# A post-norm decoder layer: head loop unrolled with batches in pairs, heads' projection and half of the feed-forward beside it

## The reference

```python
q, k, v = ((x @ W).reshape(B, T, 16, 128) for W in (Wq, Wk, Wv))     # x: 4,256,256; W: 256,2048
q, k = rmsnorm(q, q_rms_w), rmsnorm(k, k_rms_w)
s = einsum('bthd,bshd->bhts', q, k) / sqrt(128) - dist * slope[h]    # causal, slope 2**-0.5 .. 2**-8
y = rmsnorm(softmax(s) @ v, subln_w)                                 # per head
x = layernorm(x + y.reshape(B, T, 2048) @ Wproj)                     # Wproj: 2048,256
a = softmax((ctx @ xWq.T + bq) @ (ctx @ xWk.T + bk).T)               # B,256,256
x = layernorm(x + x_mixed)             # x_mixed: x_b @ a_b.T, per batch (the tokens' 256 channels mixed)
g, u = bitlinear(x, w_gate), bitlinear(x, w_up)    # 1024 wide; 8-bit activations, ternary weights
x = layernorm(x + bitlinear(sigmoid(g) * u, w_down))
```

## Time and profile before

| | |
|---|---|
| median of 3 runs | 434.68 us (433.88 to 435.26) |
| profiled execution, first to last instruction (span) | 432.9 us |
| PE busy | 401.9 us (93%) |
| DVE busy | 327.7 us (76%) |
| ACT busy | 254.4 us (59%) |
| POOL busy | 220.2 us (51%) |
| first q/k/v matmul | 18.77 us |
| last head step's matmuls | to about 312 us |
| mean granted TensorE clock | 0.979 |

### The profile page before, as it was taken

How to read it: one execution, slowest core, us unless ns; L and a number is a source line. 1 busy time by engine, 2 the same in 40 slices (tenths; PEclk the granted TensorE clock), 3 DMA queues, 4 the chain that set the end, 5 groups by cost and what they waited for, 6 DMA issues and landing times.

```text
span 432.9 us, 9595 instructions
## 1 busy us (share of the span) xinstructions
PE 401.9 (93%) x2605; PEld 361.1 (83%) x2612; DVE 327.7 (76%) x1000; ACT 254.4 (59%) x750; POOL 220.2 (51%) x368
## 2 busy tenths in 40 slices
PE   4979999999999999999999999999999899999552
PEld 3668899999999999999999999999988677777321
DVE  0777987887797798788779779878822788888862
ACT  3486777677676776767767677676722333333321
POOL 3633667676675776767767677675501122222210
PEclk9999999999999999999999999999999999999965
DMA  8980010110101101011010110000000000000000
GB/s 223 316 251 2 2 36 3 38 37 0 36 0 36 36 0 36 0 36 36 0 36 0 36 36 0 0 0 0 0 2 0 2 0 15 12 14 12 13 14 24
DMA packets 21747, 14.52 MB, mean 34 GB/s; under 512 B 1760, under 2 KB 21472, under 8 KB 21728
## 3 DMA queue, kind: packets, MB, share of 16 engines
q1 hardware_dynamic: 21728, 14.29, 11.2%
HBM read 13.24 MB, written 1.05 MB: 33 GB/s over the span
## 4 chain that ended last, share of the span: by engine, by line
PE 86%; DVE 5%; ACT 4%; issue 2%; DMA 1%; POOL 1%; SPq 0%; POOLq 0%; DVEq 0%
PE ps L482 30%; PE ps L422 11%; PE ps L493 7%; PE ps L506 6%; PE ps L499 5%; PE ps L512 4%; PE ps L505 3%; PE ps L514 3%; PE ps L513 3%; PE ps L521 3%; PE ps L587 3%; PE ps L572 2%; ACT hT L696 2%; DMA x_sb<-in_x 1%; PE ps L557 1%
## 5 line engine op out<-in xcount | busy, mean ns | idle before, releaser
L315 POOL TENSOR_TENSOR qk_rstd<-qk_sum,minus_half 128x2 f32<-128x2 f32 x128 | 88.5, 692 | 92.6 <-DVE qk_sum L797 90.8
L482 PE MATMUL ps<-w_hi,xT_hi 128*128 128x384 f32 x256 | 96.9, 378 | 2.3 <-DVE qk_n L791 1.4
L482 PE MATMUL ps<-w_hi,xT_lo 128*128 128x384 f32 x256 | 86.5, 338 | 0.0
L482 PE MATMUL ps<-w_lo,xT_hi 128*128 128x384 f32 x256 | 86.3, 337 | 0.0
L797 DVE TENSOR_REDUCE qk_sum<-sq 128x2 f32<-128x258 f32 x128 | 53.6, 419 | 30.8 <-ACT sq L635 29.1
L635 ACT ACTIVATE sq<-ps 128x256 f32<-128x256 f32 x128 | 49.1, 384 | 34.6 <-PE ps L482 34.4
L791 DVE TENSOR_TENSOR qk_n<-ps,qk_rstd 128x256 f32<-128x256 f32 x128 | 54.2, 423 | 18.8 <-POOL qk_rstd L315 17.8
L422 PE MATMUL ps<-wp,yT 128*128 128x256 f32 x256 | 62.2, 382 | 0.0
L310 POOL TENSOR_TENSOR y_rstd<-y_sum,minus_half 128x2 f32<-128x2 f32 x64 | 49.0, 766 | 24.6 <-DVE y_sum L804 20.9
L673 ACT ACTIVATE sqy<-ps 128x258 f32<-128x258 f32 x64 | 24.8, 387 | 58.5 <-PE ps L514 58.5
L422 PEld LDWEIGHTS ps<-wp,yT 128*128 128x128 f32 x256 | 46.7, 190 | 5.9
(11 more groups left out here) (126 smaller groups left out, 846.9 us busy)
## 6 DMA issues: line engine op xcount, KB each, us to landing
w_raw<-in_L_attn_Wq SPq DMA_DIRECT2D x16, 128.0 KB, 2.2
w_raw<-in_L_attn_Wk SPq DMA_DIRECT2D x16, 128.0 KB, 2.3
w_raw<-in_L_attn_Wv SPq DMA_DIRECT2D x16, 128.0 KB, 2.3
wp<-in_L_attn_Wproj SPq DMA_DIRECT2D x1, 2048.0 KB, 16.1
ff_raw<-in_L_ffn_w_gate SPq DMA_DIRECT2D x1, 1024.0 KB, 8.6
ff_raw<-in_L_ffn_w_up SPq DMA_DIRECT2D x1, 1024.0 KB, 11.0
ff_raw<-in_L_ffn_w_down SPq DMA_DIRECT2D x1, 1024.0 KB, 13.0
out<-fin SPq DMA_DIRECT2D x8, 128.0 KB, 1.7
```

The costliest lines, as they stand in the source:

```text
L315: pool.tensor_tensor(qk_rstd[:, t, :], qk_sum[:, t, :], minus_half[:], ALU.pow).then_inc(s_rs[t], 1)
L482: last = pe.matmul(ps[:, t, 0:3 * D], xa[:, k, tok], wa[:, r, k * 3 * D:(k + 1) * 3 * D], start=(i == 0), stop=(i == len(parts) - 1))
```

## The change

The loop is unrolled: every body is written out for n in 0 to 68. Step n is now head n // 2 % 16 of batch 2 * (n // 32) + n % 2, so batches 0 and 1 finish all heads at step 31 and batches 2 and 3 at step 63. Each head's weights are therefore loaded and split twice (32 groups of two steps instead of 16 of four); the high parts are now made by ACT in one copy a group (`split_hi`), the low parts by POOL.

The projection is done per four heads and batch (`quad_at`): 24 fp32r matmuls of 256 columns into PSUM region 0, twelve in each of two slots, from y and Wproj split into high and low parts; DVE adds the result onto x in SBUF (`accumulate`). For this, y^T is stored as `yT_hi` (ACT) and `yT_lo` (DVE, one more instruction each step), and `wp_lo` is made by POOL.

Everything else goes into two *slots* of a body: slot 0 stands ahead of q/k/v of tile 1 on PE, after `norm(n, 0)` on DVE and between the two qk_rstd on POOL; slot 1 stands at the end of the body on PE, and on DVE, POOL and ACT near the start of the next body, on POOL ahead of y_rstd. `plan()` gives the slots: the cross attention in steps 1 to 17, one block of feed-forward weights in each of steps 6 to 29, and from step 36 the whole feed-forward of tiles 0 to 3 (batches 0 and 1), seventeen stages a tile, a tile about every seven steps. After the bodies, five rounds remain for tiles 4 to 7. The sigmoid becomes 0.5 * (1 + tanh(g / 2)), its factors folded into scales. The prologue is cut to the transposes of x of batches 0 and 1; the first loads are x of batch 0 and, on ACT's queue, the first weights.

The schedule:

```diff
+STAGES = ("st0", "x1", "t1", "xm", "x2a", "x2b", "t2", "g0", "u0", "g1", "u1", "hs", "hr", "hq", "th", "dn", "fin")
...
+            steps = [2 * H * (b // 2) + 2 * (QUAD * k + i) + b % 2 for i in range(QUAD)]
+            if steps[-1] + 5 == n:
+                return b, k, steps
...
+    for k in range(FF_UNITS):
+        put(6 + k, 0, "fquant", k)
+        put(6 + k, 1, "fturn", k)
+    slot = 2 * 36
+    for u in range(FFN_IN_LOOP):
+        for stage in STAGES:
+            while stage in IN_PSUM and slot % 2 == 0 and quad_at(slot // 2):
+                slot += 1
+            put(slot // 2, slot % 2, stage, u)
+            if stage == "th":
+                after = slot
+            slot += 1
+        slot = after
```

The body of POOL, and its new `split_lo`:

```diff
+            def split_lo(g, piece):
+                if piece == 0:
+                    pool.wait_ge(s_whi, g + 1)
                 cols = slice(piece * KC * D, (piece + 1) * KC * D)
...
+                pool.tensor_tensor(w_lo[:, g % 3, cols], w_flat(g)[:, cols], w_hi[:, g % 3, cols].bitcast(F32),
+                                   ALU.subtract).then_inc(s_split, 1)
...
+            for n in range(STEPS + 3):
+                if n > 0:
+                    side_work(n - 1, 1)
+                if n >= 3:
                     pool.wait_ge(s_ssy, n - 2)
                     wait(pool, s_yn, n - 3)
                     pool.tensor_tensor(y_rstd[:], y_sum[:], minus_half[:], ALU.pow).then_inc(s_ry, 1)
...
+                if n < STEPS:
+                    qk_rstd_of(n, 0)
+                side_work(n, 0)
+                if n < STEPS:
+                    qk_rstd_of(n, 1)
+                g = n // 2 + 2
+                if g < GROUPS:
+                    if n % 2 == 0:
+                        split_lo(g, 0)
+                        split_lo(g, 1)
+                    else:
+                        split_lo(g, 2)
+                if n % 2 == 1 and 0 <= n // 2 - 1 < H:
+                    h = n // 2 - 1
+                    pool.wait_ge(s_wphi, h // 4 + 1)
+                    pool.tensor_tensor(wp_lo[:, h, :], wp_raw[:, h // QUAD % 2, h % QUAD, :], wp_hi[:, h, :].bitcast(F32),
+                                       ALU.subtract).then_inc(s_wplo, 1)
+
+                if n % 2 == 1 and 2 <= g - 1 < GROUPS:
+                    pool.wait_ge(s_sc, 2 * (g - 3) + 2)
+                    by = 0.5 if (g - 1) % H >= 2 else 2.0 ** (H // 2 - 1)
+                    pool.tensor_scalar(bias[:, (g - 1) % 2], bias[:, (g - 1) % 2], by, 1.0, ALU.mult,
+                                       ALU.mult).then_inc(s_bias, 1)
```

PE, the projection of four heads (t is the slot):

```diff
+                for i, m in enumerate(steps):
+                    for j, (ya, wa) in enumerate(((yT_hi, wp_hi), (yT_hi, wp_lo), (yT_lo, wp_hi))):
+                        last = pe.matmul(region[0][:, t * C:(t + 1) * C], ya[:, m % RING, t * P:(t + 1) * P],
+                                         wa[:, head_of(m), :], start=(i == 0 and j == 0),
+                                         stop=(i == QUAD - 1 and j == 2))
```

The body of DVE (the instructions that were there before, such as y_sum, y_n, pT, are unchanged):

```diff
+            for n in range(STEPS + DEPTH):
+                if 0 <= n - 1 < STEPS:
+                    norm(n - 1, 1)
+                if 0 <= n - 3 < STEPS:
                     dve.wait_ge(s_sqy, n - 2)
                     wait(dve, s_ry, n - 3)
                     dve.tensor_reduce(y_sum[:], sqy[:], AX.X, ALU.add).then_inc(s_ssy, 1)
...
+                if n > 0:
+                    side_work(n - 1, 1)
+                if n < STEPS:
+                    sums(n, 0)
+                if 0 <= n - 3 < STEPS:
                     dve.wait_ge(s_ry, n - 2)
                     wait(dve, s_ty, n - 3)
                     dve.tensor_tensor(y_n[:], ps_y[:, :, 0:D], y_rstd[:].unsqueeze(2).to_broadcast([P, TT, D]),
                                       ALU.mult).then_inc(s_yn, 1)
...
+                if 0 <= n - 2 < STEPS:
                     dve.wait_ge(s_tp, n - 1)
                     wait(dve, s_y, n - 2)
                     dve.tensor_copy(pT[:], ps_pT).then_inc(s_pT, 1)
...
+                if n < STEPS:
+                    norm(n, 0)
+                side_work(n, 0)
+                if 0 <= n - 4 < STEPS:
+                    m = n - 4
+                    dve.wait_ge(s_yhi, m + 1)
+                    dve.scalar_tensor_tensor(out=yT_lo[:, m % RING, :].rearrange("p (t d) -> p t d", t=TT), in0=ps_yT,
+                                             scalar=sub_scale,
+                                             in1=yT_hi[:, m % RING, :].bitcast(F32).rearrange("p (t d) -> p t d", t=TT),
+                                             op0=ALU.mult, op1=ALU.subtract).then_inc(s_ylo, 1)
+                if n < STEPS:
+                    sums(n, 1)
...
+            for m in range(FFN_IN_LOOP, NT + 1):
```

More of the change, by code:

```diff
@@ new lines, with plan, put @@
+IN_PSUM = ("xw", "ctx", "cq", "ck", "wtotal", "energy", "cturn", "turnx", "fturn",
+           "t1", "xm", "t2", "g0", "u0", "g1", "u1", "th", "dn")
+def plan():
+    at = {}
+    def put(n, slot, stage, i):
+        at.setdefault((n, slot), []).append((stage, i))
+    put(1, 0, "xw", 0)
+    for i in range(2):
+        put(2 + i, 0, "ctx", i)
+        put(4 + i, 0, "cq", i)
+        put(6 + i, 0, "ck", i)
+    for i in range(3):
+        put(2 + i, 1, "wsum", i)
+    put(5, 1, "wtotal", 0)
+    for b, (energy, norm, turn) in enumerate(((8, 9, 10), (9, 10, 14), (13, 14, 16), (15, 16, 17))):
+        put(energy, 0, "energy", b)
+        put(norm, 0, "cnorm", b)
+        put(turn, 0, "cturn", b)
+    put(18, 0, "turnx", 2)
+    put(21, 0, "turnx", 3)
+    for k in range(FF_UNITS):
[11 more added lines that the diff above has]
+        slot = after
+    assert slot < 2 * (STEPS + DEPTH) - 2
+    return at
@@ new lines, in gate_up, with turn_hq @@
+            def gate_up(to, w, f):
+                for k in range(KC):
+                    last = pe.matmul(to, xqT[:, k, :], w[:, k, f * BANK:(f + 1) * BANK],
+                                     start=(k == 0), stop=(k == KC - 1))
+                return last
+            def turn_hq(to):
+                for f in range(FC):
+                    last = pe.transpose(to.bitcast(BF16)[:, f * P:(f + 1) * P], hq[:, f * P:(f + 1) * P],
+                                        ident16[:])
+                return last
@@ new lines, in down, with qkv @@
+            def down(to):
+                for f in range(FC):
+                    last = pe.matmul(to[:, 0:C], hT[:, f, :], wdT[:, f, :], start=(f == 0), stop=(f == FC - 1))
+                return last
+            def qkv(n, t):
+                b, g = batch_of(n), n // 2
+                if t == 0 and n % 2 == 0:
+                    if g == 0:
+                        pe.wait_ge(s_wlo0, 1)
+                        wait_evacuated(pe, "turnx", 0)
+                    else:
+                        pe.wait_ge(s_split, SPLITS * g)
+                if t == 0 and n == 1:
+                    wait_evacuated(pe, "turnx", 1)
+                if t == 0 and n == 2 * H:
+                    wait_evacuated(pe, "turnx", 3)
+                wait(pe, s_qkn[t], n)
+                tok = slice(b * T + t * P, b * T + (t + 1) * P)
+                parts = [(xa, wa, k) for k in range(KC) for xa, wa in
+                         ((xT_hi, w_hi), (xT_hi, w_lo), (xT_lo, w_hi))]
+                for i, (xa, wa, k) in enumerate(parts):
+                    last = pe.matmul(ps[:, t, 0:3 * D], xa[:, k, tok], wa[:, g % 3, k * 3 * D:(k + 1) * 3 * D],
+                                     start=(i == 0), stop=(i == len(parts) - 1))
+                last.then_inc(s_qkv[t], 1)
@@ L522, in step @@
                     last.then_inc(s_ty, 1)
[L523 to L543 removed]
+                side_work(n, 1)
@@ new lines, in _, with x_hi, split_hi @@
+            act.wait_ge(s_table, 1)
+            act.activation(table[:], table[:], ACT.Exp)
+            def x_hi(b, of):
+                act.copy(xT_hi[:, :, b * T:(b + 1) * T], of.rearrange("p (k t) -> p k t", k=KC)).then_inc(s_xhi, 1)
+            def split_hi(g):
+                act.wait_ge(s_wraw[g % 2], 48 * (g // 2 + 1))
+                wait(act, s_qkv[1], 2 * (g - 3) + 2)
+                act.copy(w_hi[:, g % 3], w_flat(g)).then_inc(s_whi, 1)
+            wait_written(act, "turnx", 0)
```

1081 lines of the change are left out of this document (560 added, 521 removed).

## The result

The changed kernel takes 511.39 us (510.79 to 512.17), the kernel before 434.68: a ratio of 1.177, 95% interval 1.175 to 1.179. The forecast of 486 had the sign; the range of 440 to 508 missed by 3 us. The profiled execution has a span of 509.7, 25.7 over the 484 of the sum.

A forecast was written before the change was run, and what follows sets the result against it. The prediction took POOL and DVE's in-order turn around a step as the bound: 8 + 30 + 160 + 32 + 179 + 75 = 484 us, plus 1.8 from profile to runs' median, gave 486 us, range 440 to 508.

The forecast's parts named there:

- The ring: In the head steps, POOL and DVE's in-order turn sets the step: 6.30 us in steps 6 to 29, 5.09 in 30 to 35.
- The prediction's sign for PE: In the steps, PE idle, busy well under 95%, its waits ended by DVE's pT or qk_n.
- The projection: In the steps, 384 fp32r matmuls of 256 columns at 0.118 us each, a group of 24 taking 2.8 us.
- I take 0.4 a step, 2: Projection in six of steps 6 to 29: adds 0.4 us a step after cover by DVE's side work, 2 us.
- the 160: Steps 6 to 29: 24 x 6.30 = 151, cross attention 7 and projection 2, sum 160 us.
- The second half: Steps 36 to 63, with four feed-forward tiles at 45 us each: 179 us together.
- Hidden; without that lead a step would wait some 3 us.: Weight loads on SP's queue: issued some three steps, 15 us, before ACT wants them, so they cost nothing.
- I take 11.4: 34: Rounds left after the steps: 11.4 us apart, 34 us in sum, projections having cost the earlier rounds almost nothing.
- some twenty dependent instructions at 0.4 to 0.7 and 24 matmuls, 15: After step 63: the last head's chain to `accumulate` takes 15 us.
- PE stays the bound: Rival: POOL's and DVE's turn overlaps more, so PE sets the steps: 444 us, range 439 to 463, chance 0.20.
- Faster: Rival: the rounds left over overlap each other, each under 8.4 us: 428 to 433 us, chance 0.09.
- The ring holds and more is lost: Rival: table loads, fetch of the long code or side-stage waits blocking PE come on top: over 508 us, chance 0.08.

The follow-up runs named there:

- e3: Changed kernel with yT_lo moved in DVE's order from behind slot 0 to ahead of the sums of tile 0: 499.31 us against 511.4.
- e2: Changed kernel with POOL's low splits and bias done one step later, between the two qk_rstd of the next body: 515.1 us against 511.4.
- e1: Changed kernel without 352 of the 384 projection matmuls, waits and sums onto x kept: 487.67 us against 511.4.
- e8: Changed kernel with all eight feed-forward tiles in the rounds behind the heads, none in the steps: 525.83 us against 511.4.
- e6: Changed kernel with plain fp32 projection operands, one matmul for three, no yT_lo or wp_lo: 504.31 us against 511.4.
- e7: Changed kernel with q/k/v weight groups 2 and 3 and the first projection weights loaded ahead of the feed-forward weights: 501.03 us against 511.4.
- e5: Changed kernel with the feed-forward weights' quantisation moved from slot 0 to slot 1 of the step before: 504.56 us against 511.4.

## Why the prediction was right in direction and too low

**The ring: right in kind, priced too high with a block.** The plain steps came as priced: by the prediction's terms 4.85 after even and 5.33 after odd steps up to 33, and marks 32 and 33 measured 4.78 and 5.27. With a block the turns were 0.28 shorter than its terms (5.77 and 6.26 for 6.06 and 6.54). Of this, 0.22 is the quantisation. The instruction of 0.64 in the earlier trace rows ran beside a split on POOL:

```profile
272.71 0.73 POOL L280 TENSOR_TENSOR w_lo<-w_raw,w_hi 128x256 fp32r<-128x256 f32 x1
```

In its new place POOL stands idle, and it takes 0.34. That 6.26 stands so close to 6.30 is an odd turn beside a mean. e3 shows the order, not the amount of work, as the cause, and the plain steps of e2 show POOL's part; behind it lie the second ring through ACT (0.17 and 0.67), DVE's own turn at 5.3 (4.9 without the low part) and PE at 4.4. So taking one addition out gives back less than its length, which the prediction did not need but a repair would. The prediction's sign for PE, "busy well under 95%", failed in the plain steps: PE shows 98% there, and e2 and e3 still bring them from 4.78 to 4.42 with the same PE work.

**The projection: right in price, wrong in cover; the sum of the steps held by luck.** 0.12 a matmul, as taken (0.118). "I take 0.4 a step, 2" for steps 6 to 29: e1 shows 1.3 to 1.7 for each projection step, 8.4 in all, and a second step of 7.45 that no change of the ring moves. Without the projection these steps take 150.9, where the ring and the cross attention were put at 151 + 7 = 158. So the 160 is right by two errors of 6 to 7 us that offset each other.

**The second half: right in size, the ring in it not shown.** 178.0 for 179; e8 puts a tile at 8.2. The projection takes 9.7 of it (e1). But e3 gains only 2.9 there, and e6 3.7 less 3.3, so few of these steps are the ring's. What sets those steps one by one, PE at 92%, the stages' waits or DVE, no run here told apart.

**The step that failed first: "Hidden; without that lead a step would wait some 3 us."** The lead of three steps holds in the loop. At the start there is none: group 2 is wanted at 12.6, in step 0, and its load is issued behind 3 MB on the same queue. ACT waits 9.27 us and the scores, in order behind it, with it. e7, which changes the order alone, brings mark 6 9.9 us nearer of the 12.6 (10.4 in the whole time). The 4.6 us of the earlier trace rows was the time from issue to landing of a load near the head of its queue; here the place in the queue decided.

**The second: "I take 11.4: 34".** The prediction read the earlier trace rows as showing that projections between the stages "cost them almost nothing". But they had a use: in the round with projections PE was at full clock at its gates. Alone, at 0.66, a round measured 12.2 to 13.6; with useless matmuls in the gaps 10.5 to 10.8. That is 6.3 of the three rounds and 1.5 at the last, a term mis-sized by 4.3 + 0.85. The 11.86 had been one gap, with a gate at full clock at its head.

**The third: "some twenty dependent instructions at 0.4 to 0.7 and 24 matmuls, 15".** From the start of body 64 (421.6) to the last `accumulate` and its norm's first row (444.9) it is 23. The prediction counted one projection of 24 matmuls behind the last head; both batches of the pair end in neighbouring steps, so the second waits for the first's `accumulate` (440.29 to 444.27, 4.0), and tile 3's last stages stand among the last bodies (2.8, by e8). Most of the last 1.5 us is the lower clock: the first twelve matmuls of the first projection there (436.03 to 438.66, granted clock 0.68 in 436 to 440) take 2.63, where twelve take 1.51 in the steps (143.67 to 145.18).

**The rivals.** "PE stays the bound" (444) fell: the steps were longer than PE needs, and changes of order shortened them with the same work on PE. "Faster" needed rounds under 8.4; even filled ones took 10.5. "The ring holds and more is lost" is where the time fell, but not for the reasons given. The only ACT_TABLE_LOAD row stands at 2.28 us, ahead of the steps, so tanh cost none; by the Trainium skill (ScalarE: Activation LUTs, section Table sets: the hidden batching unit) exp and tanh share a set, and the trace agrees. What was lost lay at the two ends, of which the prediction gave the end -6 to +4 and the start 7 to 10.

## What to carry to other kernels

Work moved out of a latency-bound tail may leave it slower, if it was what kept TensorE at its full clock: price a tail's matmuls by rows at the clock that it will have, not that it had. In a written-out schedule look at the first time each thing happens: a load that leads by three steps in the loop may have no lead in step 0, and the queue's order then decides. And when one ring is shortened, ask for the other rings that share a part with it and for the turn of each engine in it; the next bound here lay 0.17 to 0.67 us behind.

## What the runs showed of the hardware

- A DVE tensor_scalar from SBUF to SBUF (256 columns, fp32) takes 0.29 to 0.34 alone and 0.46 to 0.83 while POOL's tensor_tensor runs (e2, e5), and L971 in e5 ends just behind the POOL instruction; beside the same w_lo, qk_n from PSUM (0.42) and the reduction y_sum (0.41) keep their time. The Trainium skill (SBUF — State Buffer, section Who interferes with whom) has the two engines share a pair of ports that one instruction holds to its end, and names tensor_scalar among those that can take it; the traces agree.
- Extra matmuls made the kernel faster: 19 of 512 columns a round raised the granted clock of the stretch from 0.66 to 0.95, and a round fell from 12.7 to 10.85 us.
- A 256-column fp32 matmul with y^T stationary goes in two passes 0.215 apart, 0.43 in all; three fp32r ones take 0.36 at full clock.
